# Attention phase of a decoder layer: the matmuls with v of a key tile are issued in the same step as its row-sum matmuls, directly ahead of them

## The chip, the cores and the metric

The kernel runs on one core of a Trainium2 chip. The time is the device time of one execution in microseconds (us), and the number compared is the median of several executions. The core has a matrix engine (TensorE, PE in the profile; its weight loads are listed apart as PEld), VectorE (DVE), ScalarE (ACT), GpSimd (POOL) and queues for transfers. Each engine takes its instructions strictly in the order of the program and stops at an instruction whose semaphore isn't there yet. What the program fixes is therefore one order for each engine; the times at which the engines meet follow from it.

## The reference, cut to what matters

The layer has three parts, one after the other: self-attention, a cross-attention without softmax ("retention"), and a feed-forward part that runs three cycles. Only the first is touched. For each of 8 batches with 512 positions and 16 heads of width 32:

```python
scores = jnp.einsum('bhqd,bhkd->bhqk', qn, kn) / np.sqrt(HD).astype(np.float32)
attn = jax.nn.softmax(scores, axis=-1)
a = jnp.einsum('bhqk,bhkd->bhqd', attn, v)
a = a.transpose(0, 2, 1, 3).reshape(b, c, dims)
return a @ out_w + out_b
```

## The kernel before

The attention phase handles 4 heads of a batch at a time. Such a **unit** U is batch U // 4, group g = U % 4; there are 32. The matrix engine works on several units at once, in one order written out by hand in `unit` (of `block.tensor`). In the pass for unit U it does the following, in 16 **steps** i = 0 to 15, after an opening part:

- `query_scores(U + 1, ..., i)`, line 686, called **q_i** here: scores of 128 queries of one head against all 512 keys, into `bank_max[i % 2]`. VectorE's `row_max`, line 437, takes the negated maximum of each row out of it. q_i waits until the maximum i-2 has been taken, since there are two banks.
- `project(U + 3, ...)`, lines 658 to 660: 48 matmuls of the projection to q, k and v, spread over steps 0 to 9.
- `key_scores(U, ..., m)`, line 701, called **k_m**: scores of 128 keys (tile kt = m // 4) of head m % 4 against all queries, with the row maximum taken off in the same product, into `bank_exp[m % 2]`. ScalarE's `exps`, line 588, turns them into probabilities (**exp m**). k_m waits until exp m-2 is done. Steps 4 to 15 issue one or two of them: k0; k1; k2, k3; k4; k5; k6, k7; and so on, two in steps 6, 9, 12 and 15.
- `weigh(U, g, kt, sums)`, line 712, twice for each key tile kt. With `sums` 0 it multiplies the probabilities of tile kt of the four heads with v, into `bank_o`: **V_kt** here. With `sums` 1 it multiplies them with ones, into `bank_sum`: **S_kt**. Each of the two is 4 matmuls in the program, one for each quarter of 32 columns of the array (`tile_position`), and 8 in the profile, where a matmul of plain f32 is two. S_kt ends with the semaphore `pv_done`, on which ScalarE waits before it overwrites the buffer of that tile two tiles later.
- For g = 0, `project_out(b - 1, t)`, lines 722 to 724: the output projection of the batch before, 12 matmuls for each t.

`WEIGH_AT` names the steps at whose end the blocks V_0, S_0, V_1, S_1, V_2, S_2 are issued. V_3 and S_3 of unit U open the pass of the next unit, followed by `make_stack` (transposes, line 673) and `transpose_max` (line 692); behind g = 0 the transposes of the next batch's input (`transpose_z`, line 648) stand ahead of V_3.

```python
                    for m in range(2 * (T - 1)):
                        if i == WEIGH_AT[m]:
                            weigh(U, g, m // 2, m % 2)
```

VectorE has an order of its own, with `row_max(U + 1, i)` in every step and other work between. In step 6 stands the long piece of `normalise` (c = 3): a reciprocal (line 449) and a product (451), then `split`, a cast of 128x512 (line 333) and a subtraction (line 335). The maximum of step 7 is behind it. `save_qkv` (lines 403, 405) follows the maxima of steps 3, 4, 8 and 10, `head_var` (419, 422) those of 3 and 9, and `n3_low` (428) those of 14 and 15.

Of the kernel before, what the change touches and what calls it, by code (L numbers as in the profile page):

```python
# [33 lines left out]
SAVE_AFTER, STATS_AFTER = (3, 4, 8, 10), (5, 8, 10, 14)  # L34
PROJECT_STEPS = 10
KEYS_FROM = 4
WEIGH_AT = (8, 9, 11, 12, 14, 15)

OUT_AT, ADD_AFTER = (12, 13, 15, 15), (11, 13, 14, 15)
HIGH_AFTER = (2, 3)  # L40
# [43 lines left out]
def attention_phase(nc, x, x1, w):  # L84
# [6 lines left out]
    with ctx:  # L91
# [542 lines left out]
        def _(pe):  # L634
# [69 lines left out]
            def weigh(U, g, kt, sums):  # L704

                if not sums:
                    pe.wait_ge(exp_done, T * HG * U + HG * (kt + 1))
                    if kt == 0 and counts(U):
                        pe.wait_ge(attn_done, U)
                for h in range(HG):  # L710
                    at = slice(h * HD, (h + 1) * HD)
                    last = mm((bank_sum if sums else bank_o)[at, :], ones[:, :] if sums else v[:, g, kt, at], probs[:, kt % 2, h, :],  # L712
                              start=kt == 0, stop=kt == T - 1, tile_position=(0, h * HD))
                if sums:
                    last.then_inc(pv_done, 1)
# [11 lines left out]
            def unit(b, g, left, first=False):  # L727
# [15 lines left out]
                for i in range(n):  # L743
# [14 lines left out]
# [3 lines that stand above are left out]
# [1086 lines left out]
```

## Time and profile before

| | |
|---|---|
| median of 3 runs | 2389.9 us (2387.33 to 2393.57) |
| span of the profiled execution | 2389.4 us; nothing outside it is listed, so it is taken as that execution's time |
| attention phase | from 0 to about 1290 us of the span |
| PE busy in 0 to 1290 us | 1105.33 us |
| DVE, ACT, POOL busy in 0 to 1290 us | 970.08, 612.24, 811.65 us |
| granted TensorE clock in 0 to 1290 us | mean 0.95 of full speed |

PE is busy for most of the attention phase, but matmuls overlap in the records, so the share says little of how much is left. What a place in the order costs is read from the times at which neighbouring matmuls start.

### The profile page before, as it was taken

Reading aid. Unit: us, or ns where it says so; the run is one execution under the profiler, and the core shown is the slowest. Engines: PE = TensorE matmul, PEld = TensorE weight load, DVE = VectorE, ACT = ScalarE, POOL = GpSimd, SP = SyncE. Lnnn points to the kernel's source line nnn. Section 1 sums busy time; section 2 is a strip of 40 time slices with the busy share of each in tenths; the row PEclk is TensorE's granted clock in tenths of the full one; section 3 lists DMA queues with packets and bytes.
Section 4 is the critical chain, followed back from the end, with each engine's and each line's share of the span. In section 5 each row is a group of like instructions: output and inputs, shape, how many; then the busy total and the mean of one; then the engine's idle time right before and its main releaser. Section 6 shows DMA issues by size and latency. Waiting matters only on the chain. (4 is left out here: it accounts for less than half of the span.)

```text
span 2389.4 us, 31918 instructions
## 1 busy us (share of the span) xinstructions
PE 1988.3 (83%) x10328; PEld 1433.3 (60%) x10328; DVE 1687.0 (71%) x3039; ACT 1043.8 (44%) x1788; POOL 1029.5 (43%) x879
## 2 busy tenths in 40 slices
PE   4579989899898998989985899999948888878772
PEld 4455655656556566556533788888736666666651
DVE  5468878788788887888773666667654777776765
ACT  1145545354453545535452222222214555555653
POOL 2567668576675766758720222222201212221121
PEclk9689999999999999999997999999979999898986
DMA  4000010100101000010004011211030121122111
GB/s 129 0 27 1 14 41 1 54 1 19 37 1 54 1 23 32 1 36 1 32 5 154 36 69 64 79 53 53 18 110 36 53 71 38 32 70 70 53 36 53
DMA packets 54719, 99.25 MB, mean 42 GB/s; under 512 B 5040, under 2 KB 8112, under 8 KB 54576
## 3 DMA queue, kind: packets, MB, share of 16 engines
q1 hardware_dynamic: 54576, 97.38, 11.9%
q8 instruction: 85, 1.39, 0.2%
q14 instruction: 58, 0.48, 0.1%
HBM read 63.82 MB, written 33.55 MB: 41 GB/s over the span
## 5 line engine op out<-in xcount | busy, mean ns | idle before, releaser
L588 ACT ACTIVATE a_probs<-a_exp 128x512 f32<-128x512 f32 x512 | 285.1, 596 | 353.6 <-PE a_exp L701 350.2
L437 DVE TENSOR_REDUCE a_neg_max<-a_max 128x1 f32<-128x512 f32 x512 | 341.1, 684 | 91.3 <-PE a_max L686 86.0
L293 POOL TENSOR_TENSOR a_rstd<-a_rstd,a_minus_half 128x16 f32<-128x16 f32 x64 | 186.3, 2911 | 189.3 <-DVE a_rstd L422 189.3
L686 PE MATMUL a_max<-a_stack 96*128 96x512 f32 x512 | 229.9, 451 | 34.2 <-DVE a_neg_max L437 34.0
L1405 POOL TENSOR_TENSOR f_mixed<-f_tw,f_beta 128x512 f32<-128x512 f32 x64 | 96.1, 1520 | 346.0 <-DVE f_beta L1504 170.1
L686 PEld LDWEIGHTS a_max<-a_stack 96*128 96x128 f32 x512 | 97.3, 191 | 173.3 <-DVE a_neg_max L437 119.7
L574 ACT ACTIVATE a_stack<-a_exp 96x512 fp32r<-96x512 f32 x256 | 138.4, 589 | 141.4 <-PE a_exp L673 140.6
L658 PE MATMUL a_t<-a_w_hi,a_zT_hi 128*128 128x384 f32 x512 | 175.8, 343 | 29.1 <-DVE a_v L405 29.1
L701 PE MATMUL a_exp<-a_stack 100*128 100x512 f32 x512 | 185.3, 404 | 2.9 <-ACT a_stack L578 2.0
L955 POOL TENSOR_TENSOR r_part<-r_part 128x512 f32<-128x512 f32 x32 | 45.8, 1431 | 313.8 <-DVE r_part L1002 313.8
L673 PE MATMUL a_exp<-a_ident,a_n 128*96 128x128 f32 x1024 | 143.1, 284 | 43.4 <-ACT a_stack L574 35.0
L659 PE MATMUL a_t<-a_w_lo,a_zT_hi 128*128 128x384 f32 x512 | 174.8, 341 | 0.0
L660 PE MATMUL a_t<-a_w_hi,a_zT_lo 128*128 128x384 f32 x512 | 174.1, 340 | 0.0
L1675 PE MATMUL f_l<-f_h_hi,f_w_hi 128*128 128x512 f32 x240 | 110.9, 462 | 72.5 <-DVE f_h_lo L1418 72.2
L673 PEld LDWEIGHTS a_exp<-a_ident,a_n 128*96 128x96 f32 x1024 | 108.8, 129 | 95.1 <-ACT a_stack L574 46.3
L449 DVE RECIPROCAL a_attn<-a_sum 128x128 f32<-128x128 f32 x128 | 122.3, 955 | 53.0 <-PE a_sum L712 50.8
L712 PE MATMUL a_o<-a_probs,a_v 128*32 128x512 f32 x1024 | 143.6, 634 | 11.4 <-DVE a_zT_lo L394 10.4
L712 PE MATMUL a_sum<-a_probs,a_ones 128*32 128x512 f32 x1024 | 142.8, 630 | 0.0
L1077 ACT ACTIVATE r_kq_hi<-r_part 128x512 fp32r<-128x512 f32 x64 | 36.8, 624 | 218.1 <-POOL r_part L956 218.1
L1418 DVE TENSOR_TENSOR f_h_lo<-f_full,f_h_hi 128x512 fp32r<-128x512 f32 x104 | 70.5, 690 | 80.4 <-ACT f_h_hi L1583 79.7
L658 PEld LDWEIGHTS a_t<-a_w_hi,a_zT_hi 128*128 128x128 f32 x512 | 98.5, 192 | 34.4 <-DVE a_v L405 29.7
L1675 PEld LDWEIGHTS f_l<-f_h_hi,f_w_hi 128*128 128x128 f32 x240 | 50.6, 211 | 105.7 <-DVE f_h_lo L1418 62.5
(239 smaller groups left out, 5299.4 us busy)
## 6 DMA issues: line engine op xcount, KB each, us to landing
a_z<-x SPq DMA_DIRECT2D x8, 1024.0 KB, 5.6
a_y<-x SPq DMA_DIRECT2D x32, 256.0 KB, 2.7
x<-a_y SPq DMA_DIRECT2D x32, 256.0 KB, 2.0
r_xn<-x SPq DMA_DIRECT2D x8, 1024.0 KB, 5.7
r_cn<-ctx SPq DMA_DIRECT2D x8, 1024.0 KB, 7.8
x<-r_xn SPq DMA_DIRECT2D x8, 1024.0 KB, 4.3
f_xn<-x SPq DMA_DIRECT2D x8, 1024.0 KB, 5.7
x<-f_xn SPq DMA_DIRECT2D x8, 1024.0 KB, 7.2
```

The costliest lines, as they stand in the source:

```text
L293: nc.gpsimd.tensor_tensor(rstd[:, c], rstd[:, c], minus_half[:, :], ALU.pow).then_inc(pool_step, 1)
L437: nc.vector.tensor_reduce(neg_max[:, t, ROW + h:ROW + h + 1], bank_max[i % 2][:, :], AX_X, ALU.max, negate=True).then_inc(max_done, 1)
L574: nc.scalar.activation(stack[0:ROW, par, j, :], bank_exp[m % 2][0:ROW, :], ACT.Copy).then_inc(stack_saved, 1)
L588: nc.scalar.activation(probs[:, kt % 2, h, :], bank_exp[i % 2][:, :], ACT.Exp, scale=float(1.0 / np.sqrt(np.float32(HD)))).then_inc(exp_do ...
L658: mm(bank, zT_hi[:, k, at], w_hi[:, k, g, :], start=k == 0, stop=False)
L659: mm(bank, zT_hi[:, k, at], w_lo[:, k, g, :], start=False, stop=False)
L660: last = mm(bank, zT_lo[:, k, at], w_hi[:, k, g, :], start=False, stop=k == K - 1)
L673: last = nc.tensor.transpose(bank_exp[c][0:ROW, t * P:(t + 1) * P], n3[:, t, h + HG * c, :, :].rearrange("p a i -> p (a i)").bitcast(F32), ...
L686: mm(bank_max[i % 2][:, :], stack[0:ROW, par, h, t * P:(t + 1) * P], stack[0:ROW, par, HG + h, :], start=True, stop=True).then_inc(score_d ...
L701: mm(bank_exp[i % 2][:, :], stack[0:ROW + HG, par, HG + h, kt * P:(kt + 1) * P], stack[0:ROW + HG, par, h, :], start=True, stop=True).then ...
L712: last = mm((bank_sum if sums else bank_o)[at, :], ones[:, :] if sums else v[:, g, kt, at], probs[:, kt % 2, h, :], start=kt == 0, stop=kt ...
L1675: mm(bank, a_hi, b_hi, start=first, stop=False)
```

## The change

One table of step numbers is another. V_0, V_1 and V_2 are issued one step later, in the step in which S_0, S_1 and S_2 already stood, and directly ahead of them.

```diff
-WEIGH_AT = (8, 9, 11, 12, 14, 15)
+WEIGH_AT = (9, 9, 12, 12, 15, 15)
```

No instruction is added or removed, and the orders of VectorE, ScalarE, GpSimd and the DMA queue are the same rows. On the matrix engine, this is steps 8 and 9 in the loop's body before, from k5 on (`a_exp`): V_0 (`a_o`), q9 (`a_max`), six matmuls of the projection (`a_t`), k6 and k7, S_0 (`a_sum`).

```order
L701 MATMUL a_exp<-a_stack 128x512
L712 MATMUL a_o<-a_probs,a_v 32x512 x4
L685 REGISTER_ALU
L686 MATMUL a_max<-a_stack 128x512
L658 MATMUL a_t<-a_w_hi,a_zT_hi 128x384
L659 MATMUL a_t<-a_w_lo,a_zT_hi 128x384
L660 MATMUL a_t<-a_w_hi,a_zT_lo 128x384
L658 MATMUL a_t<-a_w_hi,a_zT_hi 128x384
L659 MATMUL a_t<-a_w_lo,a_zT_hi 128x384
L660 MATMUL a_t<-a_w_hi,a_zT_lo 128x384
L701 MATMUL a_exp<-a_stack 128x512 x2
L712 MATMUL a_sum<-a_probs,a_ones 32x512 x4
```

And the same place with the change, again from k5 on:

```order
L701 MATMUL a_exp<-a_stack 128x512
L685 REGISTER_ALU
L686 MATMUL a_max<-a_stack 128x512
L658 MATMUL a_t<-a_w_hi,a_zT_hi 128x384
L659 MATMUL a_t<-a_w_lo,a_zT_hi 128x384
L660 MATMUL a_t<-a_w_hi,a_zT_lo 128x384
L658 MATMUL a_t<-a_w_hi,a_zT_hi 128x384
L659 MATMUL a_t<-a_w_lo,a_zT_hi 128x384
L660 MATMUL a_t<-a_w_hi,a_zT_lo 128x384
L701 MATMUL a_exp<-a_stack 128x512 x2
L712 MATMUL a_o<-a_probs,a_v 32x512 x4
L712 MATMUL a_sum<-a_probs,a_ones 32x512 x4
```

V_0 no longer stands between k5 and q9; it stands between k7 and S_0. The second place is steps 13 to 15 on the matrix engine before (q13, k12, q14, k13, V_2, q15, k14, k15, S_2); steps 10 to 12 read alike, with V_1 and S_1.

```order
L686 MATMUL a_max<-a_stack 128x512
L701 MATMUL a_exp<-a_stack 128x512
L685 REGISTER_ALU
L686 MATMUL a_max<-a_stack 128x512
L701 MATMUL a_exp<-a_stack 128x512
L712 MATMUL a_o<-a_probs,a_v 32x512 x4
L685 REGISTER_ALU
L686 MATMUL a_max<-a_stack 128x512
L701 MATMUL a_exp<-a_stack 128x512 x2
L712 MATMUL a_sum<-a_probs,a_ones 32x512 x4
```

With the change:

```order
L686 MATMUL a_max<-a_stack 128x512
L701 MATMUL a_exp<-a_stack 128x512
L685 REGISTER_ALU
L686 MATMUL a_max<-a_stack 128x512
L701 MATMUL a_exp<-a_stack 128x512
L685 REGISTER_ALU
L686 MATMUL a_max<-a_stack 128x512
L701 MATMUL a_exp<-a_stack 128x512 x2
L712 MATMUL a_o<-a_probs,a_v 32x512 x4
L712 MATMUL a_sum<-a_probs,a_ones 32x512 x4
```

Seven score matmuls now follow one another without a block between them, and two blocks follow those.

## Rows read from the trace of the kernel before

**Rows 1.** Head of the page.

```profile
span 2389.4 us, 31918 instructions
```

**Rows 2.** Who waited for whom, PE, 100 to 1290 us: total us, times, longest.

```profile
PE a_max L686 <- DVE a_neg_max L437: 34.0, 40, 2.4
PE a_exp L648 <- DVE a_z L387: 18.8, 13, 4.3
```

**Rows 3.** Timeline of PE, unit 10 (g = 2), steps 8 to 9: start, us, instruction, idle before.

```profile
513.27 1.06 PE L712 MATMUL a_o<-a_probs,a_v 128*32 128x512 f32 x8
515.36 0.50 PE L686 MATMUL a_max<-a_stack 96*128 96x512 f32 x1 [1.03 <-DVE a_neg_max L437]
...
516.76 0.63 PE L701 MATMUL a_exp<-a_stack 100*128 100x512 f32 x2
517.32 1.06 PE L712 MATMUL a_sum<-a_probs,a_ones 128*32 128x512 f32 x8
```

**Rows 4.** The same timeline, steps 10 to 12.

```profile
518.32 0.50 PE L686 MATMUL a_max<-a_stack 96*128 96x512 f32 x1
518.66 0.40 PE L701 MATMUL a_exp<-a_stack 100*128 100x512 f32 x1
518.89 0.40 PE L686 MATMUL a_max<-a_stack 96*128 96x512 f32 x1
519.13 0.40 PE L701 MATMUL a_exp<-a_stack 100*128 100x512 f32 x1
519.46 1.06 PE L712 MATMUL a_o<-a_probs,a_v 128*32 128x512 f32 x8
520.46 0.50 PE L686 MATMUL a_max<-a_stack 96*128 96x512 f32 x1
520.80 0.63 PE L701 MATMUL a_exp<-a_stack 100*128 100x512 f32 x2
521.36 1.07 PE L712 MATMUL a_sum<-a_probs,a_ones 128*32 128x512 f32 x8
```

**Rows 5.** The same timeline, from S_2 to the next unit's opening transposes.

```profile
525.39 1.06 PE L712 MATMUL a_sum<-a_probs,a_ones 128*32 128x512 f32 x8
526.48 1.06 PE L712 MATMUL a_o<-a_probs,a_v 128*32 128x512 f32 x8
527.36 1.05 PE L712 MATMUL a_sum<-a_probs,a_ones 128*32 128x512 f32 x8
528.33 1.08 PE L673 MATMUL a_exp<-a_ident,a_n 128*96 128x128 f32 x8
```

**Rows 6.** Timeline of DVE in the same unit.

```profile
511.45 1.57 DVE L333 CAST a_attnT_hi<-a_attn 128x512 fp32r<-128x512 f32 x1
513.05 1.66 DVE L335 TENSOR_TENSOR a_attnT_lo<-a_attn,a_attnT_hi 128x512 fp32r<-128x512 f32 x1
514.63 1.28 DVE L437 TENSOR_REDUCE a_neg_max<-a_max 128x1 f32<-128x512 f32 x2
...
518.86 0.69 DVE L437 TENSOR_REDUCE a_neg_max<-a_max 128x1 f32<-128x512 f32 x1 [1.02 <-PE a_max L686]
```

**Rows 7.** Timeline of ACT in the same unit.

```profile
519.09 1.08 ACT L588 ACTIVATE a_probs<-a_exp 128x512 f32<-128x512 f32 x2 [0.81 <-PE a_exp L701]
...
525.27 1.08 ACT L588 ACTIVATE a_probs<-a_exp 128x512 f32<-128x512 f32 x2 [0.94 <-PE a_exp L701]
```

**Rows 8.** Timeline, all engines, the last unit, where k_m stand alone.

```profile
1251.51 1.08 ACT L588 ACTIVATE a_probs<-a_exp 128x512 f32<-128x512 f32 x2 [0.65 <-PE a_exp L701]
...
1252.16 1.28 PE L701 MATMUL a_exp<-a_stack 100*128 100x512 f32 x2 [0.51 <-ACT a_probs L588]
```

**Rows 9.** Instructions that write a_attnT_hi or a_attnT_lo: ns min/median/max, first and last start.

```profile
L333 DVE CAST a_attnT_hi<-a_attn x32: 426/1550/1575, 184.2 to 1273.3; 128x512 fp32r<-128x512 f32 x32
L335 DVE TENSOR_TENSOR a_attnT_lo<-a_attn,a_attnT_hi x32: 691/1656/1671, 185.8 to 1273.7; 128x512 fp32r<-128x512 f32 x32
```

**Rows 10.** Timeline of POOL in unit 10.

```profile
511.43 1.30 POOL L298 TENSOR_TENSOR a_n<-a_n,a_head_w 128x512 f32<-128x512 f32 x1
512.81 1.35 POOL L300 TENSOR_TENSOR a_n<-a_n,a_head_b 128x512 f32<-128x512 f32 x1
```

## The prediction, made before the changed kernel ran

> **What bounds the kernel now.** I read the list of waits first, then the timelines of the three engines over one unit, side by side. Unit 10 is taken, whose pattern the others repeat. The attention phase is paced by PE, which stands still in a few places only. The largest wait that concerns this change is that of query scores for a row maximum: 34.0 us in 40 waits, about one per unit [rows 2]. Its place is step 9. q9 starts at 515.36, 1.03 us after the matmuls ahead of it ended [rows 3]. It needs a free bank, so maximum 7, and VectorE reaches that only at 514.63, behind the cast of 1.57 us and the subtraction of 1.66 us that close `normalise` [rows 6]; it ends about 0.68 later, at 515.31. So q9 starts when VectorE lets it. What PE does between k5 and q9 is free up to that moment, and before the change it does V_0 there.
>
> Elsewhere PE runs on without a wait: steps 10 to 12 follow at fixed distances [rows 4]. These distances are the prices I use. A score matmul follows another after 0.23 or 0.24 (518.66, 518.89, 519.13). A block in column quarters between them costs more than its own work: 0.33 from the matmul before it (519.13 to 519.46), 1.00 to the next full-array matmul (519.46 to 520.46), and 0.34 instead of 0.23 behind that one (520.46 to 520.80) [rows 4]. Where one block follows another it starts 0.88 later (526.48 to 527.36), and the transposes start 0.98 behind that one's start [rows 5].
>
> **The change, part by part.** Nothing is added, and no queue but PE's is changed. Three blocks for each unit move behind other PE work, so there are three terms, and one at the unit's end.
>
> *Steps 8 and 9.* V_0 leaves the gap ahead of q9. VectorE's chain up to maximum 7 takes nothing from V_0, so it ends when it did, and q9 stays at 515.36. PE only waits longer: V_0's 1.00 us joins the wait of 1.1 us. From q9 to k7 all is as before. V_0 now starts where S_0 did, and S_0 0.88 later [rows 5]. Cost: **+0.88 us**, since the cover is gone. Bounds: 0.88 if the stall covered V_0 wholly; with no stall it would be 0.88 less the 1.00 and the transition of some 0.2, that is -0.3.
>
> *Steps 10 to 12.* Before, S_0 to S_1 takes 521.36 - 517.32 = 4.04 us [rows 3, 4]. With V_1 gone to the end, S_0 1.00, q10 0.34, then q11, k9, q12, k10, k11 and V_1, all behind k8 at distances of 0.24 and the last of 0.33, would bring V_1 at 2.87 and S_1 at 3.75: -0.29 us, the price of two changes of array mode. But k10 and k11 wait for exps 8 and 9, as V_1 no longer gives ScalarE that time. k8 starts at 1.34; its exp starts 0.43 later (518.66 to 519.09 [rows 4, 7]), and two exps take 1.08, one of them 0.59, so they start 0.49 apart [rows 7]. How fast PE follows is seen in the last unit: exps start at 1251.51, the first ends at 1252.10 and the next matmul starts at 1252.16 [rows 8]. So exp 8 runs from 1.77 to 2.36, exp 9 to 2.85. A matmul whose weight load was held up starts 0.05 to 0.15 behind its exp. That gives k10 at about 2.5 and k11 at about 3.0, V_1 at 3.33 and S_1 at 4.21 to 4.22. q12 waits for maximum 10 as well: VectorE starts it 0.54 behind q10 (518.32 to 518.86 [rows 4, 6]), it ends at 2.23, sooner than exp 8, so it isn't what binds. Cost: **+0.18 us**, between -0.29 (the exps never bind) and +0.35 (another 0.15 or so of exposed weight load).
>
> *Steps 13 to 15.* The same order and the same two chains, V_2 for V_1: **+0.18 us**. `n3_low` is between the last two maxima on VectorE, and nothing of PE in this stretch waits for them.
>
> *From S_2 on.* Before, V_3 starts 1.09 behind S_2 (525.39 to 526.48) since it waits for exp 15, which ends at 525.27 + 1.08 = 526.35 [rows 5, 7]. Now V_2 stands between k15 and S_2, exp 15 is done early, and V_3 follows after 0.88: **-0.21 us**.
>
> A usual unit thus gets longer by 0.88 + 0.18 + 0.18 - 0.21 = 1.03 us. There are 21 of them. In 7 units (g = 0) the output projection stands in steps 12, 13 and 15. Steps 14 and 15 there go from q14 to S_2 in 0.23 + 0.32 + 1.00 + 0.34 + 0.23 + 0.33 = 2.45 us before, and with the change in 0.23 (k13) + 0.43 + 0.59 + 0.15 (exp 13, then k15) + 0.33 + 0.88 = 2.61: +0.16. Nothing comes back at their end, where the transposes of the next input wait for VectorE (18.8 us in 13 waits [rows 2]) ahead of V_3. So they get 0.88 + 0.18 + 0.16 = 1.22 us. The other four, the first and the last three units, I put at 4 us together, between 0 and 7. The first has no `normalise` and so hardly a stall (about 0). The last has no query scores, so ScalarE paces it and each V block covered a wait (about 1.4). One between runs partly at half clock, where a block costs nearly double.
>
> Sum: 21 x 1.03 + 7 x 1.22 + 4 = 34.2 us. On the span of 2389.4 [rows 1] that is 2423.6; the median of the runs shown lies 0.5 above the span, which gives **2424 us**, 1.4% slower. The two other phases share no instruction with this.
>
> **The rivals.**
>
> *The saved mode changes are kept (no wait for exps).* If k10, k11, k14 and k15 find their banks free, a usual unit changes by 0.88 - 0.29 - 0.29 - 0.21 = +0.09 us, and the total by some +5 us: 2395, within or just over what can be told from no change. For it speaks that k10 and k11 wait nowhere today [rows 4]; against it that an exp takes 0.59 and the four scores between two blocks come 0.24 to 0.48 apart.
>
> *Only the mode changes count (faster).* If q9 were not tied to maximum 7 and the exps never bound, each of the three pairs would save 0.29 and the end 0.21: 1.08 us per unit, some 30 us in all, 2360. Against it stands the end of maximum 7 at 515.31 with q9 at 515.36 [rows 3, 6].
>
> The Trainium skill has a rule on that side: the page "TensorEngine Tiling (Array Packing)", Key Properties, says that a change of tiling mode (not of the tile alone) drains the engine. The trace agrees, with 0.29 us for a block set beside another; by the rule alone the change could only gain.
>
> *VectorE's long piece shrinks (faster).* The cast and the subtraction have medians of 1.55 and 1.66 us, but minima of 0.43 and 0.69 [rows 9]. In unit 10 the cast starts at 511.45, just behind a GpSimd operation at 511.43, and ends near 513.02, when that one has ended at 512.73 and the next is already under way; the subtraction again spans the next one [rows 6, 10]. If the change shifted the two engines against each other so that both ran short, maximum 7 would come up to 2.1 us sooner. From a gain of about 1.03 us per unit on, the change would be even. With the whole 2.1 us, of which PE without V_0 could use nearly all, it is about -1.1 us per unit, -30 us: 2360. Against it: both engines are set off by `head_var` in step 3 of the same unit, and nothing ahead of step 8 moves, so the 0.02 us between them should stay.
>
> The Trainium skill bears on that rival: "SBUF — State Buffer", SBUF: two separate sides, says that a VectorE operation of a two-port mode and a GpSimd operation exclude one another for the whole instruction. The stretched operations beside GpSimd's agree. By it the stall falls only if the order of arrival turns.
>
> *More than forecast.* Weight loads held up behind waits are exposed in full at every one of the four waits, and the loss in each run of scores is 0.35 or more: +45 us, 2435.
>
> **How the numbers follow.** What a measurement of this kernel can tell from no change is about 0.3%, 7 us. My forecast, +24 to +42 us, gets 0.74 and has 2414 to 2432 as its own range. Partial forms of it (part of the stall or of the exp waits fails to show, +8 to +24) get 0.08; the mode changes kept, near +5, 0.07; the mode changes alone, 0.01; the shorter long piece, 0.04; more than +42, 0.06. The range must leave out no more than 2 in 10: it is 2402 to 2434. Slower by over 0.3%: 0.74 + 0.08 + 0.06 = 0.88, of which I take 0.02 off to "same" for the lower edge of the partial forms. Same: 0.09. Faster: 0.05.
>
> **What the changed profile would show.** PE's wait for `a_neg_max` about 1 us longer per unit, so some 60 us instead of 34.0. V_0 starting 0.33 behind k7 and S_0 0.88 behind V_0, with q9 still tied to the end of maximum 7. A new wait of PE at line 701 for `a_probs`, about 0.46 us at each of two places per unit, where there is none now. V_3 0.88 behind S_2. The cast still near 1.55 us. The step most likely to be wrong is the wait behind the exps: if S_0 to S_1 is 3.75 and not 4.2 us, the first rival holds. If q9 comes sooner after k5 than now, the stall's cause was read wrongly.

## The result and the profile after

The changed kernel takes 2459.74 us (2459.07 to 2462.7, 4 executions) against 2390.22 for the kernel before: 1.0288 times as long, 95% interval 1.0276 to 1.0301. That is 69.5 us slower. I had forecast slower, by 34 us, with 2434 as the upper end; the loss is twice as large.

Head of the page of the changed kernel.

```profile
span 2458.5 us, 31918 instructions
```

The list of waits of PE from 100 to 1370 us: who waited for whom, total us, times, longest. It answers to [rows 2].

```profile
PE a_max L686 <- DVE a_neg_max L437: 64.7, 47, 3.7
...
PE a_exp L648 <- DVE a_z L387: 24.4, 7, 4.6
...
PE a_exp L701 <- ACT a_probs L588: 3.3, 13, 0.5
```

The wait for row maxima grew from 34.0 to 64.7 us, about as forecast (some 60). The forecast new wait of key scores for exps, about 0.46 us at two places of each unit, isn't there in that form: it is 3.3 us in 13 waits, after 0.9 in 3 before. What holds k10 and k11 instead is taken up in the experiments. The timeline of PE in unit 10 answers to [rows 3 to 5]: k5, q9, the first and the last of the six matmuls of the projection, k6 and k7, V_0, S_0, and steps 10 to 12. Two weight loads (PEld) that waited stand in their places.

```profile
534.93 0.39 PE L701 MATMUL a_exp<-a_stack 100*128 100x512 f32 x1
537.30 0.50 PE L686 MATMUL a_max<-a_stack 96*128 96x512 f32 x1 [1.99 <-DVE a_neg_max L437]
537.64 0.44 PE L658 MATMUL a_t<-a_w_hi,a_zT_hi 128*128 128x384 f32 x1
...
539.16 0.52 PE L660 MATMUL a_t<-a_w_hi,a_zT_lo 128*128 128x384 f32 x1
539.48 1.05 PE L701 MATMUL a_exp<-a_stack 100*128 100x512 f32 x2
540.46 1.38 PE L712 MATMUL a_o<-a_probs,a_v 128*32 128x512 f32 x8
541.66 1.03 PE L712 MATMUL a_sum<-a_probs,a_ones 128*32 128x512 f32 x8
542.62 0.50 PE L686 MATMUL a_max<-a_stack 96*128 96x512 f32 x1
542.96 0.40 PE L701 MATMUL a_exp<-a_stack 100*128 100x512 f32 x1
543.21 0.40 PE L686 MATMUL a_max<-a_stack 96*128 96x512 f32 x1
543.44 0.40 PE L701 MATMUL a_exp<-a_stack 100*128 100x512 f32 x1
543.91 0.19 PEld L686 LDWEIGHTS a_max<-a_stack 96*128 96x128 f32 x1 [0.51 <-DVE a_neg_max L437]
543.91 0.50 PE L686 MATMUL a_max<-a_stack 96*128 96x512 f32 x1
544.25 0.79 PE L701 MATMUL a_exp<-a_stack 100*128 100x512 f32 x2
544.54 0.19 PEld L701 LDWEIGHTS a_exp<-a_stack 100*128 100x128 f32 x1 [0.30 <-ACT a_probs L588]
544.97 1.06 PE L712 MATMUL a_o<-a_probs,a_v 128*32 128x512 f32 x8
545.85 1.04 PE L712 MATMUL a_sum<-a_probs,a_ones 128*32 128x512 f32 x8
```

PE idles for 1.99 us ahead of q9, where it idled 1.03 before. What I had not in the sum comes right behind: a matmul of the projection takes 0.52 us, one follows the other after 0.32 instead of 0.18, and from q9 to V_0 it takes 3.16 us (537.30 to 540.46), where q9 to S_0 took 1.96 before [rows 3]. Three stretches of the same unit say why. The columns are the busy time of PE, PEld, DVE, ACT and POOL, each with its instructions in brackets, then the granted clock as a share of full speed, and the DMA.

```profile
534.90:537.74 2.84, 0.85 (x5) 0.44 (x4) 2.81 (x4) 0.60 (x1) 1.20 (x1) 1.00 0.00 0
537.74:541.20 3.46, 3.46 (x13) 2.27 (x15) 2.00 (x6) 1.06 (x2) 1.35 (x1) 0.51 0.00 0
541.20:544.00 2.80, 2.73 (x21) 1.01 (x13) 0.84 (x2) 0.62 (x3) 2.64 (x3) 1.00 0.00 0
```

The granted TensorE clock of the second stretch, just behind the emptied stall, is 0.51 of full speed, which is the lower of its two levels (1.2 GHz); in the third stretch it is 1.00 again (2.4 GHz).

How much a whole unit grew is seen from the starts of `transpose_max` in successive units, in us; a median over the five or six units of the loop of each kind:

| kernel | g = 1 | g = 2 | g = 3 | g = 0 |
|---|---|---|---|---|
| before | 31.24 | 31.44 | 31.24 | 53.85 |
| changed | 32.17 | 33.88 | 33.72 | 57.21 |
| growth | 0.93 | 2.44 | 2.48 | 3.36 |

Units with g = 1 grew by 0.93 us, near the 1.03 of the forecast; the clock stays up in six of the seven (the first of them, unit 1, has the drop and takes 33.7 us). Units with g = 2 and 3 grew by 1.5 us more, and those with g = 0 by 3.4 instead of 1.22. The times of g = 0 are the least certain: their ends run partly at half clock in every kernel, and from V_3 to `transpose_max` they take 4.2 to 5.3 us within one execution of the kernel before.

### The profile page after: what moved, and what is told of

Read it like the earlier page. It is cut to its first block and busy times, and to the rows that moved or that the text cites. A ratio compares the mean times of both kernels' runs of the same rounds, so it can differ in the third digit from the quotient of the medians.

```text
span 2458.5 us, 31918 instructions
## 1 busy us (share of the span) xinstructions
PE 2020.2 (82%) x10328; PEld 1467.6 (60%) x10328; DVE 1687.6 (69%) x3039; ACT 1044.9 (43%) x1788; POOL 1020.8 (42%) x879
## 5 line engine op out<-in xcount | busy, mean ns | idle before, releaser
L686 PE MATMUL a_max<-a_stack 96*128 96x512 f32 x512 | 228.7, 449 | 68.8 <-DVE a_neg_max L437 64.7
L701 PE MATMUL a_exp<-a_stack 100*128 100x512 f32 x512 | 206.0, 437 | 5.3 <-ACT a_probs L588 3.3
L659 PE MATMUL a_t<-a_w_lo,a_zT_hi 128*128 128x384 f32 x512 | 180.3, 352 | 0.0
L660 PE MATMUL a_t<-a_w_hi,a_zT_lo 128*128 128x384 f32 x512 | 179.8, 351 | 0.0
L712 PE MATMUL a_o<-a_probs,a_v 128*32 128x512 f32 x1024 | 155.2, 682 | 10.4 <-DVE a_zT_lo L394 10.4
L701 PEld LDWEIGHTS a_exp<-a_stack 100*128 100x128 f32 x512 | 102.6, 202 | 37.3 <-ACT a_probs L588 28.6
```

Of the source, the lines that this page charges most:

```text
L659: mm(bank, zT_hi[:, k, at], w_lo[:, k, g, :], start=False, stop=False)
L660: last = mm(bank, zT_lo[:, k, at], w_hi[:, k, g, :], start=False, stop=k == K - 1)
L686: mm(bank_max[i % 2][:, :], stack[0:ROW, par, h, t * P:(t + 1) * P], stack[0:ROW, par, HG + h, :], start=True, stop=True).then_inc(score_d ...
L701: mm(bank_exp[i % 2][:, :], stack[0:ROW + HG, par, HG + h, kt * P:(kt + 1) * P], stack[0:ROW + HG, par, h, :], start=True, stop=True).then ...
```

## The experiments

My theory after the result: the moved V_0 costs its 0.88 us as forecast; the stall without V_0 lets the clock fall, for 1.5 us more in most units; V_1 and V_2 cost little; something at the end of the g = 0 units costs 1.1. The main rival: the missing part comes from V_1 and V_2.

**V_0 alone, and V_1 and V_2 alone.**

```diff
-WEIGH_AT = (8, 9, 11, 12, 14, 15)
+WEIGH_AT = (9, 9, 11, 12, 14, 15)
```

> Only V_0 moves, from step 8 to step 9; V_1 and V_2 stay where they were before the change. Theory A (the lost cover and the clock): V_0 costs 0.88 us in each of about 29 units, some 26 us, and the stall of 2.2 to 2.5 us that is left ahead of q9 without any matmul lets the granted clock fall to 0.5 in about 22 units, for 1.5 us each, some 33 us. So about +59 us on the kernel before, 2449, with granted-clock drops in step 9 as in the changed kernel. Theory B (the clock drops come from the waits that V_1 and V_2 leave behind k9 and k13, or what is missing is lost at the ends of the units with g = 0): +26 us, 2416, and no clock drop in step 9.

Measured: 2456.42 us, ratio 1.0273 (1.0256 to 1.0290), +65 us where I gave +59. Units take 32.33, 34.11, 33.93 and 56.57 us for g = 1, 2, 3 and 0. Nearly the whole loss is V_0's, with the clock drops where the changed kernel has them.

```diff
-WEIGH_AT = (8, 9, 11, 12, 14, 15)
+WEIGH_AT = (8, 9, 12, 12, 15, 15)
```

> Only V_1 and V_2 move, to steps 12 and 15; V_0 stays in step 8. Theory A: each of the two runs of scores costs 0.15 us net (S_0 to S_1 4.19 instead of 4.04 us) and the unit's end gives 0.23 back, +0.05 to +0.1 us per unit, +2 us, and up to 8 us more if the ends of the 7 units with g = 0 get longer by 1.1 us each as they did in the changed kernel: 2392 to 2400. No clock drop in step 9. Theory B: +35 us or more, 2425.

Measured: 2403.41 us, ratio 1.0049 (1.0032 to 1.0066). Units with g = 1, 2, 3 take 31.31, 31.53 and 31.32 us, 0.07 to 0.09 more than before; those with g = 0 take 55.85, 2.0 more. There is no clock drop in step 9. So the total was a little above what I gave, and lies almost wholly in the g = 0 units. The two parts, +65 and +12, come to 77, and together they cost 69.5. A difference of that size shows in the units' ends: with V_0 alone, V_3 to `transpose_max` takes 3.05 us in units with g = 1, where it took 2.77 before and takes 2.75 with all three moved, and g = 2 and 3 read alike. No run tests why.

**Something to do in the stall.** The changed kernel, with a copy of V_0 in step 8 that nobody uses.

```diff
-            def weigh(U, g, kt, sums):
+            def weigh(U, g, kt, sums, alone=False):
...
-                              start=kt == 0, stop=kt == T - 1, tile_position=(0, h * HD))
+                              start=kt == 0, stop=alone or kt == T - 1, tile_position=(0, h * HD))
...
+                    if i == 8:
+                        weigh(U, g, 0, 0, True)
```

> The changed kernel with a useless copy of V_0's matmuls in step 8, where V_0 stood; the real V_0 overwrites its result in step 9. It adds 32 times 8 matmuls of 592 ns to PE's work. Theory A: the copy lies wholly in the stall ahead of q9, PE isn't idle there for over 1.2 us, the granted clock stays up in step 9 and the time falls to what the distances alone give, 2420 to 2432, some 33 us under the changed kernel, although PE does more. Theory B: more work on PE and the same waits: 2460 or more.

Measured: 2433.47 us, ratio 1.0181 (1.0164 to 1.0198), a little above my 2432, and 26 us less than the changed kernel, with 256 matmul records more. Timeline of PE in unit 10: k5, the copy, q9, k6 and k7, V_0, S_0.

```profile
525.59 0.39 PE L701 MATMUL a_exp<-a_stack 100*128 100x512 f32 x1
525.91 1.06 PE L712 MATMUL a_o<-a_probs,a_v 128*32 128x512 f32 x8
528.02 0.50 PE L686 MATMUL a_max<-a_stack 96*128 96x512 f32 x1 [1.04 <-DVE a_neg_max L437]
...
529.42 0.63 PE L701 MATMUL a_exp<-a_stack 100*128 100x512 f32 x2
529.97 1.06 PE L712 MATMUL a_o<-a_probs,a_v 128*32 128x512 f32 x8
530.86 1.04 PE L712 MATMUL a_sum<-a_probs,a_ones 128*32 128x512 f32 x8
```

A stretch of it, in the columns of the stretches above:

```profile
528.51:531.90 3.39, 3.39 (x26) 1.59 (x24) 1.95 (x6) 1.08 (x2) 1.32 (x1) 1.00 0.00 0
```

q9 still starts 2.43 us behind k5 (2.37 in the changed kernel), so the copy takes no time of its own. q9 to V_0 is 1.95 us again and the clock 1.00. Units take 32.18, 32.38, 32.19 and 56.48 us: g = 2 and 3 give back the 1.5 us that g = 1 had not lost, and g = 0 gives back 0.7.

**A quarter of it.** The same copy for one head only.

```diff
-                for h in range(HG):
+                for h in range(1 if alone else HG):
```

> The changed kernel with a useless copy of a quarter of V_0 (one head of four, 2 matmul records of 592 ns instead of 8) in step 8. Theory A as far as the full copy showed: what counts is that PE does something in the stall. Two matmuls over one quarter of the array keep it busy for about the same 1 us, so the granted clock stays up in step 9 and the time is that with the full copy, 2433. Theory B: the clock follows how much of the array works, a quarter isn't enough, the drops stay and the time is 2460.

Measured: 2428.98 us, ratio 1.0164 (1.0148 to 1.0179). Two matmul records on a quarter of the array keep the clock up as well as eight do. What counted here was that PE did something in the stall. With either copy PE's longest idle time ahead of q9 in the loop is 1.2 us, as in the kernel before, and the clock in step 9 is 1.00 in every unit there.

**The end of the g = 0 units.** V_1 and V_2 moved alone, and one small memset on GpSimd.

```diff
+        pad = sb("pad", [P, 1])
...
                 if g == 0 and left == 4:
                     x_rstd(b + 1)
+                    nc.gpsimd.memset(pad[:, :], 0.0)
```

> V_1 and V_2 moved alone, V_0 in step 8, as in the run before, plus one memset of 128x1 on GpSimd behind x_rstd in units with g = 0, which starts GpSimd's following operations about 0.1 us later. Theory A (the ends of the units with g = 0 got longer because VectorE's n3_low now starts 0.02 us behind a GpSimd operation instead of 0.10 ahead of it, and takes 1.27 us instead of 0.68): n3_low starts first again, S_2 to the transposes of the next input takes 9.0 us again instead of 10.1, and the time falls by 7 us, to about 2396. Theory B (the longer end comes from the later S_2 itself): nothing changes, 2403.

Measured: 2396.67 us, ratio 1.0025 (1.0014 to 1.0036). The timeline of VectorE and GpSimd near the end of such a unit, first in the kernel before:

```profile
303.27 0.68 DVE L428 TENSOR_TENSOR a_n<-a_n 128x512 fp32r<-128x512 f32 x1
303.37 1.19 POOL L279 TENSOR_TENSOR a_turn<-a_qk,a_sin 128x256 f32<-128x256 f32 x1
```

With V_1 and V_2 moved, without the memset:

```profile
303.77 0.75 POOL L279 TENSOR_TENSOR a_turn<-a_qk,a_sin 128x256 f32<-128x256 f32 x1
303.79 1.27 DVE L428 TENSOR_TENSOR a_n<-a_n 128x512 fp32r<-128x512 f32 x1
...
306.85 0.66 DVE L384 SCALAR_TENSOR_TENSOR a_shift_x<-a_moments,a_rstd_x 128x4 f32<-128x4 f32 x1
```

And with it (the added lines shift the line numbers by up to 2):

```profile
305.08 1.29 POOL L280 TENSOR_TENSOR a_turn<-a_qk,a_sin 128x256 f32<-128x256 f32 x1
305.08 0.68 DVE L430 TENSOR_TENSOR a_n<-a_n 128x512 fp32r<-128x512 f32 x1
...
307.56 0.15 DVE L386 SCALAR_TENSOR_TENSOR a_shift_x<-a_moments,a_rstd_x 128x4 f32<-128x4 f32 x1
```

In the kernel before, `n3_low` (L428) starts 0.10 us ahead of GpSimd's operation and takes 0.68 us. With V_1 and V_2 moved, GpSimd's starts 0.02 us ahead and VectorE's takes 1.27 us; the changed kernel reads alike, with 0.02 to 0.05 us and 1.25 to 1.27. With the memset the two starts are recorded less than 0.02 us apart, VectorE's takes 0.68 again and GpSimd's is the long one; against the other it moved by these 0.02 us only, not by the 0.1 that I had expected. The small operation L384 takes 0.66 us where a GpSimd operation starts 0.09 ahead of it and 0.15 where one starts 0.04 behind it. This chain ends in the next input, for which PE waits. From S_2 to the transposes of that input it is 9.01 us in the kernel before, 10.13 in the changed one, 10.14 with V_1 and V_2 moved alone, and 8.98 with the memset. Part of that is made up again within the transposes: V_3 follows S_2 after 15.98, 16.82, 16.83 and 15.94 us. So 0.9 us of each unit comes back, 6 us in 7 units, and the time fell by 6.7, or by 5.7 if the two ratios are compared. The memset was tried with V_0 in step 8 only, not in the changed kernel itself.

The Trainium skill describes such a lock in "SBUF — State Buffer", SBUF: two separate sides: of a VectorE operation with two inputs in SBUF and a GpSimd operation that reads SBUF, whichever starts first has the shared ports for its whole instruction. These rows agree, down to who is the long one when the order turns.

**What V_1 and V_2 wait for.** Exps on half their columns (the other half of the probabilities isn't computed).

```diff
-                    nc.scalar.activation(probs[:, kt % 2, h, :], bank_exp[i % 2][:, :], ACT.Exp,
+                    nc.scalar.activation(probs[:, kt % 2, h, 0:S // 2], bank_exp[i % 2][:, 0:S // 2], ACT.Exp,
```

> V_1 and V_2 moved alone, V_0 in step 8, and every exp on the first 256 of its 512 columns only; the other half of the probabilities isn't computed. An exp then takes about 0.38 us instead of 0.59. Theory A (what the moved V_1 and V_2 lose is the wait of k10, k11, k14 and k15 for exps): S_0 to S_1 falls from 4.19 us to between 3.75 and 3.85, and a usual unit gets 0.6 to 0.8 us shorter than with the full exps, 2380 to 2390. Theory B (the wait is for row maxima, or for weight loads): S_0 to S_1 stays above 4.1.

Measured: 2385.51 us, ratio 0.9984 (0.9975 to 0.9993), and S_0 to S_1 4.06 us instead of 4.22 (medians over 22 units). I had missed: short exps give back 0.16 us and not 0.4, and a usual unit gets 0.32 us shorter (30.99 after 31.31 for g = 1), not 0.6 to 0.8. That the time fell within my 2380 to 2390 is luck: at the ends of the g = 0 units `n3_low` went back to 0.68 us, and these units got 2.1 us shorter. Then the maxima cut in half, with whole exps, and both cut:

```diff
-                nc.vector.tensor_reduce(neg_max[:, t, ROW + h:ROW + h + 1], bank_max[i % 2][:, :], AX_X, ALU.max,
+                nc.vector.tensor_reduce(neg_max[:, t, ROW + h:ROW + h + 1], bank_max[i % 2][:, 0:S // 2], AX_X, ALU.max,
```

> V_1 and V_2 moved alone; row_max reads the first 256 of its 512 columns only, so the maxima are those of half the keys. A row maximum takes about 0.42 us instead of 0.68, all over VectorE, so only distances between the blocks are compared and not the time. Theory A (q12 waits for maximum 10 and so holds k10, and k11 waits for exp 9 a little later; either of the two alone costs nearly the whole 0.44 us): q12 follows k9 at 0.24 instead of 0.47, but k10 and k11 then wait for exps 8 and 9, and S_0 to S_1 stays at 4.10 to 4.20 us. Theory B (only the maxima bind): S_0 to S_1 3.75.

> Both cuts together: exps and row maxima on 256 of 512 columns, V_1 and V_2 moved alone. Theory A: with neither chain binding, steps 10 to 12 run at PE's own distances, S_0 to S_1 3.75 to 3.80 us, against 4.07 with short exps alone and 4.19 with neither. Theory B (weight loads or the change of array mode keep the scores apart): S_0 to S_1 stays above 4.0.

Measured: S_0 to S_1 4.22 us with short maxima, 4.00 with both, where I gave 4.10 to 4.20 and 3.75 to 3.80. (One execution each, 2378.56 and 2354.66 us after 2389.22 for the kernel before.) The timeline of PE with both cut, unit 2, from S_0 to S_1, with one weight load:

```profile
218.33 1.06 PE L712 MATMUL a_sum<-a_probs,a_ones 128*32 128x512 f32 x8
219.33 0.50 PE L686 MATMUL a_max<-a_stack 96*128 96x512 f32 x1
219.66 0.40 PE L701 MATMUL a_exp<-a_stack 100*128 100x512 f32 x1
219.90 0.40 PE L686 MATMUL a_max<-a_stack 96*128 96x512 f32 x1
220.14 0.40 PE L701 MATMUL a_exp<-a_stack 100*128 100x512 f32 x1
220.38 0.47 PE L686 MATMUL a_max<-a_stack 96*128 96x512 f32 x1
220.68 0.84 PE L701 MATMUL a_exp<-a_stack 100*128 100x512 f32 x2
221.02 0.19 PEld L701 LDWEIGHTS a_exp<-a_stack 100*128 100x128 f32 x1 [0.29 <-ACT a_probs L588]
221.45 1.06 PE L712 MATMUL a_o<-a_probs,a_v 128*32 128x512 f32 x8
222.34 1.04 PE L712 MATMUL a_sum<-a_probs,a_ones 128*32 128x512 f32 x8
```

Up to q12 the scores now come at 0.24 (220.14 to 220.38), where q12 came 0.47 behind k9 in the changed kernel (543.44 to 543.91). So q12 did wait for maximum 10. k10 and k11 stay slow (220.68 to V_1 0.77, where 0.57 were due), and the weight load of k11 waits for exp 9 even here. The distances from k9 on tell the two causes apart (medians over units with g = 1, 2, 3, in us):

| V_1 and V_2 moved, and | k9 to q12 | q12 to k10 | k10 to k11 | k11 to V_1 | sum |
|---|---|---|---|---|---|
| nothing else | 0.47 | 0.34 | 0.29 | 0.43 | 1.53 |
| short exps | 0.47 | 0.34 | 0.24 | 0.33 | 1.38 |
| short maxima | 0.24 | 0.37 | 0.49 | 0.43 | 1.53 |
| both short | 0.24 | 0.31 | 0.33 | 0.43 | 1.31 |
| no wait (forecast's distances) | 0.24 | 0.24 | 0.24 | 0.33 | 1.05 |

With short exps only maximum 10 binds, for 0.33 us. With short maxima only the exps bind, for the whole 0.48: taking the maxima away alone gives nothing back. With both short, k11 still starts 0.05 us behind the end of exp 9, as an exp starts 0.44 us behind its matmul and takes 0.38 even when cut. So the run with both cut is not the clean test that it was meant to be, and the 0.25 us that remain of 4.00 are the wait of k11 (0.09) and the late starts behind the two matmuls whose weight loads were held up (0.07 for k10, 0.10 for V_1).

**The other direction.**

```diff
-WEIGH_AT = (8, 9, 11, 12, 14, 15)
+WEIGH_AT = (8, 8, 11, 12, 14, 15)
```

> The other direction: V_0 and S_0 both in step 8, ahead of q9; V_1, S_1, V_2, S_2 as before the change. Theory A: the stall of 2.1 us ahead of q9 holds V_0 (1.00) and nearly all of S_0 (0.88 more), so q9 keeps its time; S_0 leaves the stretch behind k7, of which the waits of k8 and k9 for exps 6 and 7 give part back: -0.7 us for each of 29 units, -20 us, 2370. Theory B: q9 gets later by the whole of S_0, and the time is the same as before or slower.

Measured: 2375.61 us, ratio 0.9932 (0.9915 to 0.9948), faster than both kernels. Timeline of PE in unit 9: k5, V_0, S_0, q9, k6 and k7, q10, k8.

```profile
480.56 0.39 PE L701 MATMUL a_exp<-a_stack 100*128 100x512 f32 x1
480.88 1.07 PE L712 MATMUL a_o<-a_probs,a_v 128*32 128x512 f32 x8
481.76 1.04 PE L712 MATMUL a_sum<-a_probs,a_ones 128*32 128x512 f32 x8
482.78 0.50 PE L686 MATMUL a_max<-a_stack 96*128 96x512 f32 x1
...
484.16 0.63 PE L701 MATMUL a_exp<-a_stack 100*128 100x512 f32 x2
484.63 0.39 PE L686 MATMUL a_max<-a_stack 96*128 96x512 f32 x1
485.25 0.50 PE L701 MATMUL a_exp<-a_stack 100*128 100x512 f32 x1 [0.23 <-ACT a_probs L588]
```

The stall takes both blocks: q9 starts 2.22 us behind k5 here and 2.20 before in a unit of this kind (2.49 after 2.42 for g = 2, 2.31 after 2.20 for g = 3). k8 then waits for exp 6, which gives part of it back. Units with g = 1, 2, 3 get 0.6 to 0.7 us shorter. Those with g = 0 are 0.55 us longer in the profiled execution, which at 2382.95 us was the slowest of the four.

**Every S block moved up.**

```diff
-WEIGH_AT = (8, 9, 11, 12, 14, 15)
+WEIGH_AT = (8, 8, 11, 11, 14, 14)
```

> Every S block moved up to stand directly behind the V block of its tile: V_0, S_0 in step 8, V_1, S_1 in step 11, V_2, S_2 in step 14. Theory A (distances and waits decide, not the adjacency): the first pair gains as it did alone, but seven scores without a block between S_1 and V_2 wait for exps, and with no block behind k15, V_3 waits for exp 15, some 1 us per unit in all more than with S_0 moved alone: 2400 to 2410. Theory B (each pair set together saves its change of array mode): 2360 or less, as the first pair gave 16 us.

Measured: 2399.09 us, ratio 1.0037 (1.0024 to 1.0050), just under the 2400 to 2410 of theory A. Units with g = 1, 2, 3 take 31.68, 31.88 and 31.69 us, 1.05 to 1.2 us more than with S_0 moved alone; those with g = 0 take 53.12, 0.7 less than before. The waits of PE, 100 to 1290 us, have a new row:

```profile
PE a_o L712 <- ACT a_probs L588: 24.4, 24, 1.0
```

V_3 waits 1 us for exp 15, as no block stands behind k15. Each of the three pairs stands side by side here, at the 0.88 us of the forecast, and with the second and the third moved as well the gain of the first is gone.

## Why the prediction was right and wrong

**The stall ahead of q9 was read rightly.** q9 stayed tied to the end of maximum 7, the wait for maxima doubled, and the lost cover costs what was given: units with g = 1 take 32.18 us with all three blocks moved and a filler, 31.31 with V_1 and V_2 moved alone, a difference of 0.87 us for V_0 (forecast 0.88). With V_0 moved alone the same units lose 1.10, 0.28 of it at the unit's end.

**The step that failed** is in steps 8 and 9, "From q9 to k7 all is as before." I had priced the matmuls behind the stall at the distances of a unit whose clock never fell. With V_0 gone from the stall, the granted clock falls to the level of 1.2 GHz behind it in g = 2, 3 and 0, which costs 1.5 us in units with g = 2 and 3 and 0.7 in those with g = 0 (57.21 against 56.48 with the copy in the stall). Filling the stall takes the ratio from 1.0288 to 1.0181 or 1.0164, that is 26 to 30 us. This is the larger part of the error of 35 us.

**A second term was missing:** at the end of the g = 0 units I wrote that nothing comes back, and gave nothing for the way there. S_2 to the next input's transposes takes 1.1 us longer, S_2 to V_3 0.84: VectorE's `n3_low` now starts 0.02 to 0.05 us behind a GpSimd operation where it started 0.10 ahead, some 6 us in all. I had named this mechanism, but for the cast in step 6 only, where it indeed didn't change (the cast took 1.56 us in unit 10 of the changed kernel). The sum closes within its uncertainty: 34.2 forecast, 26 to 30 for the clock, some 6 for these ends, 66 to 70 against 69.5 measured.

**The price of V_1 and V_2 was right in size and half wrong in cause.** S_0 to S_1 is 4.19 us in the changed kernel (forecast 4.21 to 4.22) and V_3 follows S_2 after 0.86 (forecast 0.88). But "so it isn't what binds", said of maximum 10, was wrong: q12 starts at 2.25 us behind S_0, right behind maximum 10, and k10 follows it 0.34 later at 2.59, while exp 8 is long done (0.25 us). k11 does wait for exp 9, as forecast. The size came out all the same, since the exps alone hold the scores for the whole 0.48 us (the run with short maxima).

**The rivals.** A change between blocks and full-array matmuls has a price, 0.12 us at the seam of two blocks (0.88 instead of 1.00) and more around it. That fits the rule of the Trainium skill in "TensorEngine Tiling (Array Packing)", Key Properties, that changing the tiling mode drains the engine; how much of the price is a drain and how much a late weight load, no run here separates. The saving went into waits each time except where a stall was free to be filled.

## What to carry to other kernels

A block that stands in a stall costs nothing there, and moved out of it behind other work it costs its length (0.87 us here); before moving one, ask which stall it fills, and look for a second block that fits in too (S_0 did, for 0.7%). An emptied stall costs more than its cover where the matrix engine then runs on at half clock, so read the granted clock of the stretch behind the longest idle time, and not only the idle time. Where two engines start operations within some hundredths of a us of each other, a shift of one order elsewhere can turn who goes first, and a run with a small pad on one of them shows whether that is where the time went. Where two chains end close together, shortening one alone shows little; read from the weight loads which one each matmul waited for.

## What the runs showed of the hardware that I had not expected

In unit 10 the granted clock fell behind a gap in which PE idled for 1.99 us, with matmuls close on both sides; with two matmul records in that gap, on a quarter of the array, it didn't fall. In unit 26, where q9 waited for 0.75 us only, it stayed up in the changed kernel too, and behind the 1.03 and 1.17 us of the kernel before it never fell. Units with g = 1 have the same gap of 1.8 us (2.2 between the starts of k5 and q9) as those with g = 3. In the changed kernel six of the seven in the loop kept the clock and unit 1 lost it; with V_0 moved alone all seven kept it; g = 3 lost it every time in both. What decides between them stays open.
